# A language model layer on one core: q is made nearly one step ahead of k, and the steps of all engines are reordered

## The reference, cut to what matters

```python
h = tok(x)                                   # x: 16 sequences of 256 tokens, h: 16 x 256 x 128
h = h + attn(layernorm(h))
h = h + ffn(layernorm(h))

# tok: nesting depth and segment of each token (both by cumulative sums over the sequence),
#      concat(position row, nesting row, segment row) @ W
# attn, for 8 heads of 64 and chunks of 128 tokens:
q, k, v = split(x @ w_qkv.T); q = q * 64 ** -0.5
q_prime = exp(q @ proj.T - max over the 64 features)      # the same for k
context = k_prime.T @ v                                   # within a chunk
out = (q_prime @ context) / (q_prime @ k_prime.sum(0) + 1e-4)
# ffn: 8 experts, the two best of each token:
gates = softmax(x @ Wg + bg); vals, idx = top_k(gates, 2); vals = vals / (vals.sum() + 0.01)
out = sum over the two of  vals * (relu(x @ W1[e] + b1[e]) @ W2[e] + b2[e])
```

## Time and profile before

| | |
|---|---|
| time, median of 3 runs | 401.78 us (400.83 to 405.43) |
| profiled execution, its own time | 401.69 us |
| its span, first to last instruction | 399.9 us |
| busy share | PE 85%, PEld (weight loads) 73%, DVE 78%, ACT 62%, POOL 60% |
| instructions | 11561 |
| mean granted TensorE clock | 0.96 of full speed |

### The profile page before, as it was taken

How to read it: one execution, slowest core, us unless ns; L and a number is a source line. 1 busy time by engine, 2 the same in 40 slices (tenths; PEclk the granted TensorE clock), 3 DMA queues, 4 the chain that set the end, 5 groups by cost and what they waited for, 6 DMA issues and landing times. The chain is left out here.

```text
span 399.9 us, 11561 instructions
## 1 busy us (share of the span) xinstructions
PE 339.1 (85%) x2966; PEld 292.0 (73%) x2966; DVE 310.1 (78%) x1186; ACT 249.3 (62%) x664; POOL 239.6 (60%) x484
## 2 busy tenths in 40 slices
PE   1948999999899988989888786699999999996860
PEld 0725777776776766777667676699999999996850
DVE  6487888888987888888899688988778777774532
ACT  2324777787676786776876655276777677773540
POOL 5011143778888777887787777655555555575350
PEclk9985999999999999999999999899999999999995
DMA  5075501000000000000000212422222222259925
GB/s 148 27 224 139 166 3 61 30 16 16 32 31 31 24 16 24 30 30 29 16 16 32 76 53 81 123 73 80 71 79 71 76 70 77 70 103 214 266 84 164
DMA packets 32030, 29.69 MB, mean 74 GB/s; under 512 B 4573, under 2 KB 27448, under 8 KB 31992
## 3 DMA queue, kind: packets, MB, share of 16 engines
q1 hardware_dynamic: 24056, 14.76, 13.6%
q0 software_dynamic: 4928, 12.59, 11.1%
q10 hardware_dynamic: 3008, 1.89, 1.6%
HBM read 16.50 MB, written 12.73 MB: 73 GB/s over the span
## 5 line engine op out<-in xcount | busy, mean ns | idle before, releaser
L720 POOL DMA_INDIRECT y_dram<-heads_out,place x72 | 74.6, 1036 | 60.6 <-ACT heads_out L892 56.0
L695 POOL DMA_INDIRECT slots_dram<-rows,row_id x64 | 63.3, 989 | 19.5 <-issue 18.9
L883 ACT ACTIVATE k_prime<-ps_out,b_T 128x128 f32<-128x128 f32 x108 | 32.0, 366 | 21.5 <-PE ps_out L1622 21.5
L800 ACT ACTIVATE k_prime<-k_prime,rstd 128x512 f32<-128x512 f32 x32 | 23.1, 722 | 33.0 <-DVE k_prime L1007 33.0
L1632 PE MATMUL ps_vc<-w_tile,k_prime 128*128 128x128 f32 x288 | 39.2, 280 | 4.9 <-issue 3.4
L883 ACT ACTIVATE k_prime<-ps_q,b_T 128x128 f32<-128x128 f32 x108 | 31.8, 365 | 17.0 <-PE ps_q L1622 16.8
L1632 PE MATMUL ps_oy<-w_tile,k_prime 128*128 128x128 f32 x288 | 38.9, 279 | 1.8 <-ACT k_prime L883 1.8
L1622 PE MATMUL ps_out<-sT,w_tile 128*128 128x128 f32 x288 | 39.6, 282 | 1.0 <-DVE w_tile L1350 1.0
L1632 PEld LDWEIGHTS ps_vc<-w_tile,k_prime 128*128 128x128 f32 x288 | 35.8, 196 | 5.4 <-issue 3.5
L1526 PE MATMUL ps_out<-context,qT 128*128 128x130 f32 x256 | 37.3, 289 | 0.5 <-ACT context L818 0.3
L1346 DVE COPY w_tile<-w_all 128x640 f32 x72 | 36.4, 506 | 1.4
(11 more groups left out here) (268 smaller groups left out, 890.9 us busy)
## 6 DMA issues: line engine op xcount, KB each, us to landing
qkv_rows<-slots_dram SPq DMA_DIRECT2D x72, 72.0 KB, 1.9
h<-y_dram POOLq DMA_DIRECT2D x4, 768.0 KB, 9.4
w_all<-in_L_ffn_W SPq DMA_DIRECT2D x1, 2048.0 KB, 14.1
w_all<-in_L_ffn_W SPq DMA_DIRECT2D x8, 256.0 KB, 4.5
y_dram<-heads_out,place POOLq DMA_INDIRECT x72
slots_dram<-rows,row_id POOLq DMA_INDIRECT x64, 2.3
qkv_rows<-in_L_attn_w_qkv ACTq DMA_DIRECT2D x1, 768.0 KB, 5.9
out<-h SPq DMA_DIRECT2D x1, 768.0 KB, 6.1
```

What stands on the lines that cost most here:

```text
L695: nc.gpsimd.indirect_dma_start(slots_dram[:, :], bass.IndirectOffsetOnAxis(row_id[:, place_of(p, a), j, k:k + 1], 0), rows[:, place_of(p, ...
L720: nc.gpsimd.indirect_dma_start(y_dram[:, :], bass.IndirectOffsetOnAxis(place[:, a, :], 0), y[:, a, :], None).then_inc(s_placed[a], 16)
L800: nc.scalar.activation(k_prime[:, a, :], k_prime[:, a, :], ACT.Exp, scale=rstd[:, b, a:a + 1])\
L883: last = nc.scalar.activation(hT[:, a % 2, c, :], ps_up[a % 2][0][:, c * P:c * P + P], ACT.Relu, bias=b1_T[:, bass.ds(experts[0] * FC + c, ...
```

## The change

Parts, all in the attention stage and just behind it:

1. **q one step ahead.** In the step of tile t, VectorE and TensorE now make k of tile t+1 and q of tile t+2. Before, both were of tile t+1. In a step, TensorE runs `context_product` first, then the k product, then the q product.
2. **Order of all engines.** TensorE: `embed` and `rank_product` now stand behind `out_product` (the ranks behind `v_product` too), `x2_transpose` behind the q product of the odd step, and `gate_product` at its end. ScalarE: `normalize_second` now opens the odd step, ahead of `context_copy`, and `exps_of` goes one step later. VectorE: ranks and choices are spread between larger instructions; `choose` and the moments of the second norm move from the odd step to the next pair's even step.
3. **The one-hot difference** (`change_of`) is made on VectorE instead of GpSimd.
4. **Joint norm scales.** One function `scale` on GpSimd takes the variances of the first norm of pair p+2 and of the second norm of pair p-1 in one add and one power over four columns. The shift is made as minus the mean, times the scale. `weigh` folds its epsilons into one product ahead of the tree of sums, so that three small instructions go and one comes.
5. **Waits on single instructions.** `step.add` returns the count, and `step.until(count)` waits for that instruction alone and not for all that came behind it.

```diff
@@ Steps
         instruction.then_inc(self.sem, 1)
         self.count += 1
+        return self.count
+
+    def until(self, count):
+
+        self.eng.wait_ge(self.sem, self.base + count)
...
@@ GpSimd
+            def scale(p, a):
+
+                first, second_norm = live(p + 2), live(p - 1)
+                part = slice(0 if first else 2, 4 if second_norm else 2)
+                count = part.stop - part.start
+                if first:
+                    pool.wait_ge(s_mom, p + 3)
+                    wait(pool, s_vo, 2 * p + 2)
+                if second_norm:
+                    pool.wait_ge(s_mom2, p)
+                    wait(pool, s_xhat2, p - 2)
+                step.done(nc.gpsimd.tensor_tensor(rstd[:, a, part], moments[:, a, part, 1], ln_eps[:, 0:count], ALU.add))
+                last = nc.gpsimd.tensor_tensor(rstd[:, a, part], rstd[:, a, part], minus_half[:, 0:count], ALU.pow)
+                if second_norm:
+                    step.add(last)
+                    step.done(nc.gpsimd.tensor_tensor(shift2[:, a, :], zero[:, :], moments[:, a, 2:4, 0], ALU.subtract))
+                    last = nc.gpsimd.tensor_tensor(shift2[:, a, :], shift2[:, a, :], rstd[:, a, 2:4], ALU.mult)
+                last.then_inc(s_norm, 1)
...
                 pool.wait_ge(s_exps, p + 1)
-                terms, width = exps, E // 2
+                step.done(nc.gpsimd.tensor_tensor(partial[:, :, :], exps[:, :, :], denom_by[:, :, :], ALU.mult))
+                width = E // 2
...
-                step.done(nc.gpsimd.tensor_tensor(denom[:, :], partial[:, :, 0], top_eps[:, :], ALU.mult))
-                step.done(nc.gpsimd.tensor_tensor(denom[:, :], denom[:, :], exps[:, :, 1], ALU.add))
-                step.done(nc.gpsimd.tensor_tensor(denom[:, :], denom[:, :], one[:, :], ALU.add))
-                step.done(nc.gpsimd.tensor_tensor(weight[:, :, 0], denom[:, :], minus_one[:, :], ALU.pow))
+                step.done(nc.gpsimd.tensor_tensor(weight[:, :, 0], partial[:, :, 0], minus_one[:, :], ALU.pow))
...
-                if live(p + 2):
-                    change_of(p + 2, a)
-                    scale_first(p + 2, a)
                 if isinstance(p, int) and p == 1:
                     make_padding()
-                if live(p - 1):
-                    scale_and_shift(p - 1, 1 - a, moments2, rstd2, shift2, s_mom2, s_rstd2)
+                scale(p, a)
...
@@ ScalarE, in a step
+                    more = live(t + 1, TILES)
+                    if j == 1 and live(p - 2):
+                        wait(act, s_slots[a], 16 * 2 * TOP * (half - 1))
+                        normalize_second(p - 2, a)
+                    if live(p):
+                        context_copy(t, j)
+                    if more:
+                        q_exp(t + 1, np_, nb, 1 - j)
+                    if j == 0 and live(p - 3):
+                        exps_of(p - 3)
...
@@ VectorE
+            def change_of(p, a):
+
+                dve.wait_ge(s_hot, p + 1)
+                nc.vector.tensor_tensor(change[:, a, :], one_hot[:, a, P:P + S], one_hot[:, a, 0:S], ALU.subtract)\
+                    .then_inc(s_change, 1)
...
                 if more:
-                    head_max(t + 1, ps_k, 1, s_k)
-                if more or ranks:
-                    step.wait()
-                if more:
-                    subtract_max(t + 1, 1, ps_k, k_prime, 1, s_c, s_ks)
-                if ranks:
-                    give_rows(p - 3, 1 - a)
+                    k_found = head_max(t + 1, ps_k, 1, s_k)
+                if choice:
+                    step.until(before_pair)
+                    chose = choose(p - 3)
+                if more:
+                    step.until(k_found)
+                    subtract_max(t + 1, 1, ps_k, k_prime, 1, s_c, s_ks)
+                if choice:
+                    step.until(chose)
+                    mark()
+                if live(p - 2):
+                    moments_of(1 - a, stats2, 2, s_mom2)
+                if q_more:
+                    q_found = head_max(t + 2, ps_q, 0, s_q)
+                if live(p):
+                    summed = divisor(t)
+                if choice:
+                    ranked = read_ranks(p - 3)
...
@@ TensorE, in a step
-                    if more:
-                        q_product(t + 1, np_, na, nj)
                     if live(p):
                         context_product(t, j)
+                    if more:
+                        k_product(t + 1, na, nj)
+                    if live(t + 2, TILES):
+                        q_product(t + 2, p + 1, 1 - a, j)
+                    if j == 1 and live(p - 2):
+                        x2_transpose(p - 2, a)
+                    if live(t - 1, TILES):
+                        o_transpose(t - 1, 1 - j)
+                    if live(p):
+                        out_product(t, j)
```

More of the change, by code:

```diff
@@ L1043, in find_top @@
                     last = nc.vector.max(top[:, j, :], logits[:, j, :])
-                step.add(last)
+                return step.add(last)
             def find_top_ids():
@@ L1123, in odd @@
                 if live(p + 2):
                     embed(p + 2, a)
-                if more:
-                    step.wait()
-                if live(p - 1):
-                    dve.wait_ge(s_h2, 2 * p)
+                if live(p):
+                    summed = divisor(t)
                 if live(p + 2):
                     dve.wait_ge(s_h, p + 3)
-                if more:
-                    subtract_max(t + 1, 0, ps_q, q_prime, 0, s_qT, s_qs)
-                    head_max(t + 1, ps_k, 1, s_k)
@@ L1164, in odd @@
                     residual(t - 1)
                 if live(p - 2):
-                    choose(p - 2)
+                    found = find_top()
+                if live(p + 2):
+                    moments_of(a, stats, 0, s_mom)
+                if live(p - 2):
+                    step.until(found)
+                    below_top(p - 2)
+                    find_top_ids()
             def weigh_last(p, a):
@@ L1198, in gates @@
                 find_top_ids()
-                below_top()
+                below_top(p)
                 step.wait()
                 choose(p)
+                step.wait()
+                mark()
             by_group = tile_expert[:, :].rearrange("p (g r) -> p g r", r=RING)
@@ L1305, in sequence @@
             def sequence(p, a, half):
+                even(p, a)
                 if isinstance(p, int) and p == -1:
@@ L1323, in _ @@
             sequences(dve, step, sequence, 30)
+            step.wait()
+            choose(SEQS - 3)
+            moments_of(1, stats2, 2, s_mom2)
+            step.wait()
+            mark()
             dve.wait_ge(s_groups, 1)
```

196 lines of the change are left out of this document (78 added, 118 removed).

## The result

| | before | after |
|---|---|---|
| time, median | 402.37 us (400.83 to 405.43, 4 runs) | 384.67 us (383.90 to 384.89, 4 runs) |
| ratio, 95% interval | 1 | 0.9548 (0.9489 to 0.9607) |
| profiled execution, and its span | 401.69 us, 399.9 us | 383.9 us, 382.0 us |
| busy share PE, DVE, ACT, POOL | 85, 78, 62, 60% | 87, 80, 65, 57% |

The changed kernel is 17.7 us faster. The forecast was 384.5 us. The total agrees, but the terms of the sum do not all, and the experiments show that one reason I gave was wrong.

What follows compares the result with a forecast made beforehand. No engine fills an attention pair; a ring of waits between TensorE, VectorE and ScalarE holds it, with GpSimd's 12.19 us a further limit. 13 x 1.2 plus 1.6 us off 401.7 gives 384.5 us, range 379 to 396.5.

Steps and rivals of the forecast that it cites:

- handoffs: Attention, per pair: 0.2 to 0.4 us added because a ring of three engines needing 10.2 to 10.6 us never closes fully.
- the loop's turns: Attention's hardware loop: its turns add 0.25 us a pair, as before the change.
- the one named as a way to fail: Stretch from 226 to 257.5 us: counted zero, give or take 1.5; the prediction fails if the gain is lost there.
- GpSimd as a second limit: Attention: GpSimd runs 12.19 us a pair without waiting for another engine, so removing the waits alone would soon meet it.
- the lightening: GpSimd in attention: difference moved off, norms joined, weights shortened; 12.19 us a pair falls to 10.1 to 10.6.
- 0.61 us free and 0.72 held: VectorE's 512-column instructions: a wait on a result just made costs 0.11 us; seven fewer a pair save 0.8 us.
- The wait for the ranks: VectorE, even step: a new wait for the ranks' product behind output and v products, 0.2 to 0.5 us a pair.
- ScalarE's wait for k: Loop's five pairs: ScalarE's wait for VectorE's k should fall to under half of 11.4 us.
- A: Attention, partial gain: GpSimd or VectorE gives back half, a pair takes 11.4 us, total 392.9 us; chance 0.25.
- B: Attention, no change: ScalarE's second-norm rows wait about 1.2 us a pair for `scale`; 401 to 402 us; chance 0.08.
- C: Attention, slower: late scatters delay `scale`, GpSimd's round exceeds 12.3 us; 407 us at 12.6 a pair; chance 0.08.
- D: Attention, more gain: handoffs cost nothing, a pair takes 10.4 us, total 378.5 us; chance 0.07.

Runs made afterwards that it cites:

- e_tail: Changed kernel with the scales of pair 15 between two halves of a scatter and the last scales ahead of pair 13's weights: 386.72 us, ratio 0.9611.
- e_before_light: Kernel before with only the one-hot difference on VectorE and the short chain of weights on GpSimd: 406.17 us, ratio 1.0090.
- heavy_again: Changed kernel with the one-hot difference back on GpSimd, behind its scatter, and the longer chain of weights: 407.09 us, ratio 1.0161.
- four variants: Changed kernel with waits for everything (430.52 us), difference on GpSimd (426.18), long chain of weights (430.28), or both latter (431.40); kernel before there 422.61.

## Why the prediction was right, point by point

**The pair.** Forecast 10.8 us unrolled and 0.25 more in the loop; measured 10.63 and 0.07 more. The terms for handoffs (0.2 to 0.4) and for the loop's turns were too large. The prediction had VectorE and GpSimd as the engines with the least slack and TensorE at some 10.2 us; in the trace it is TensorE, busy 10.56 us of 10.63, that the others keep up with. From the first to the last divided tile attention fell from 185.87 us (39.39 to 225.26) to 164.25 (37.87 to 202.12), by 21.6 us and not 17.2.

**Start-up and tail.** Both were to be zero, give or take 1.5. Start-up gained 1.5, at the edge. The tail lost 5.1 us, outside, and this was the mis-sized term, the one named as a way to fail. The sum gave it nothing since "the moved choice and mask are the same instructions at another place". GpSimd in the changed kernel around the last divide (202.12), with VectorE's row numbers of pair 12:

```profile
197.35 0.19 POOL L656 TENSOR_TENSOR rstd<-moments,ln_eps 128x2 f32<-128x2 f32 x1 [1.69 <-DVE moments L989]
...
199.19 0.18 DVE L1082 TENSOR_REDUCE row_id<-chosen_at 128x4 int32<-128x32 f32 x1
...
202.37 1.06 POOL L691 DMA_INDIRECT slots_dram<-rows,row_id  x1 [0.29 <-issue]
...
206.28 1.12 POOL L691 DMA_INDIRECT slots_dram<-rows,row_id  x1 [0.30 <-issue]
```

The same in the kernel before, around its last divide (225.26):

```profile
219.50 0.17 DVE L1079 TENSOR_REDUCE row_id<-chosen_at 128x4 int32<-128x32 f32 x1
...
220.50 1.06 POOL L695 DMA_INDIRECT slots_dram<-rows,row_id  x1 [0.49 <-issue]
...
224.40 0.96 POOL L695 DMA_INDIRECT slots_dram<-rows,row_id  x1 [0.30 <-issue]
```

Pair 12's scatters end at 207.40, 5.3 us behind the start of the last divide. In the kernel before they ended at 225.36, level with it. The other chip's two traces agree: 5.3 us behind it (208.48 against 203.19), and 0.1 (224.59 against 224.49). From the end of these scatters to the expert tiles at full pace it is 32.1 us in both kernels (207.40 to 239.50, 225.36 to 257.50). So the 5.1 us are there before the tail begins. Two moves of the change stand at their source. The choice went one step later, so that the row numbers of pair 12 come 2.8 us ahead of the last divide and not 5.6. And the joint scale waits 1.69 us for moments, ahead of the weights in GpSimd's queue. How the delay divides between them no run shows. Nor is the clock parted from it, which is 0.70 from 227 to 239.5 us, where TensorE is busy 8.1 of 12.5 us. e_tail shows that the order of the last norms is not what holds the tail. Which of the last 16 scatters could be earlier was not tried.

So the way was right, and the closeness of the total (384.5 against 384.67) is luck: 4.4 us more in attention and 1.5 in start-up stand against 5.1 in the tail.

**GpSimd as a second limit.** Here the reason was wrong. I read 12.19 us without a wait for another engine as what GpSimd needs, and the lightening as room for its round. e_before_light freed 1.3 us a pair and won nothing. With q's lead, undoing the lightening costs 22 us, 21 of them by the difference behind the scatters. Its 0.68 us would make GpSimd's round 11.1 us by length, 5 us over the whole, and not 21. The prediction moved the difference to shorten GpSimd's round; it missed that q's lead calls for its input earlier, and that this made the move to VectorE necessary.

**VectorE.** 0.61 us free and 0.72 held: confirmed at 0.60 and 0.70 by the same instruction in two kernels. By the time the single waits are worth 5.4 us. The Trainium skill ("VectorE: DVE Perf Modes", section "The DRAIN you can't avoid") reports eight copies that took as long without semaphores between them as with them. Carried over to this kernel that would have made the single waits worth nothing, and the runs do not agree. The same section adds that an instruction that is not held starts earlier, which the prediction left out and which is what these runs show. `change` takes 0.29 us, 0.21 from start to start, at the low end of 0.2 to 0.7 and not the 0.3 that I took. The wait for the ranks, 0.2 to 0.5 a pair forecast, appeared twice in the whole trace, for 0.8 us together.

**The other signs.** The four-column power at 1.04 us lies in 0.7 to 1.2, the joint norm's 1.8 in 1.45 to 2.0. ScalarE's wait for k fell to nothing in those pairs. The expert stage kept its 124.5 us. GpSimd waited for moments in two of three unrolled pairs (0.5 us together) and in the five of the loop no wait is put down to them.

**The rivals.** A (392.9 us) asked for one meeting of VectorE and GpSimd a pair at up to 0.7 us. Single ones are there: GpSimd's `partial` took 0.37 us at 144.70 and 0.22 in other pairs. They are short, and the pair is not longer for them. B's place is real: ScalarE's rows waited for the shift six times in five pairs, but 0.6 us at most and not 1.2. The prediction had named such a wait in every pair as a sign of failing; it came and the time held, so as a sign it lacked a size. C decided at a GpSimd round of 12.3 us; heavy_again is such a kernel (12.7 us a pair), and its 407.1 us are C's 407, by another mechanism. D had 10.4 us a pair, and the pairs took 10.63.

## What to carry to other kernels

An engine that shows no wait for another engine may still not set the pace; take a piece of its work away, and if it starts to wait, it was only being paced. When an operation is moved ahead in time, list the inputs that it now needs earlier and which queue each stands in: here one 0.68 us instruction behind four scatters cost 21 us. A stop of TensorE can cost more than its length, since the clock may be lower behind it (1.94 us instead of 1.06 for the same product). What is moved to a later step of a steady stage also comes out of that stage later, so the stretch behind it needs a term of its own in the sum.

## What the runs showed of the hardware that was not expected

The kernel before took 401.6 to 402.4 us in four sets of runs and 422.6 us in one, on another chip. No trace of it was taken on the slower chip, nor was the changed kernel run there, so whether its gain holds on such a chip stays open. The slower chip's traces are of four variants. In the one that waits for everything, TensorE, GpSimd, ScalarE and VectorE in an even step ("remote" is a releaser that the profile has no record of):

```profile
142.60 0.69 PE L1533 MATMUL ps_vc<-v_ones,k_prime 128*64 128x65 f32 x16
...
144.65 0.95 POOL L691 DMA_INDIRECT slots_dram<-rows,row_id  x1 [0.30 <-issue]
146.50 0.38 ACT L809 ACTIVATE context<-ps_vc 64x260 f32<-64x260 f32 x1 [4.40 <-remote]
146.53 0.69 DVE L1000 TENSOR_REDUCE qk_max<-ps_k 128x8 f32<-128x512 f32 x1 [2.18 <-remote]
...
147.33 2.10 PE L1543 MATMUL ps_out<-context,qT 128*128 128x130 f32 x8 [2.90 <-ACT context L810]
```

ScalarE's context copy starts 3.9 us behind the product that it reads, where the same kernel on another chip shows 0.73 in even steps, and VectorE's k maximum is released in the same moment. The output product then takes 2.10 us instead of 1.06. In each of the four variants ScalarE's context copy waits in this way six to eight times between 70 and 215 us, 22 to 33 us in all and up to 4.9 at once. In the rows shown a scatter runs on GpSimd meanwhile; whether it has a part in it was not tested. The granted clock is between 0.83 and 1.00 in stretches of 30 us from 70 to 220 us here; these are means over times at 2.4 and at 1.2 GHz. On the other chips it is 1.00 throughout attention in six of the kernels, and below that in the two with the difference back on GpSimd. Whether the late starts bring the lower clock or the other way round, these traces do not decide, and a third to a half of the semaphore events are missing from them. That two chips give one variant opposite signs (0.9717 and 1.0163) means that a comparison needs both kernels on the same chip and, where it matters, more than one chip.
